# Chunk steps of an RWKV-and-experts kernel cut at another place: the shared down projection, ranks and scatter of a chunk finished in the step after

## The reference, cut to what matters

```python
def wkv(w, u, k, v):                      # a scan over time, per channel
    def step(carry, kv_t):
        aa, bb, pp = carry
        ...
        y = (e1 * aa + e2 * vt) / (e1 * bb + e2)
        ...
xk = xn * att_mix_k + xx * (1.0 - att_mix_k)          # xx: xn one token earlier; xv, xr alike
k, v = xk @ Wk.T, xv @ Wv.T
rwkv = sigmoid(xr @ Wr.T) * wkv(time_decay, time_first, k, v)
x = x + rwkv @ Wo.T
kf = square(relu(xk2 @ Wk_ffn.T))                     # channel mix, 256 -> 1024
x = x + sigmoid(xr2 @ Wr_ffn.T) * (kf @ Wv_ffn.T)
...
shared = (gelu(xf @ w1s) * (xf @ w2s)) @ w3s          # for all tokens
idx = argmax(xf @ Wg, axis=-1)                        # one of 8 experts for each token
final[t] = (gelu(xf @ W1[idx]) * (xf @ W2[idx])) @ W3[idx]
out = x + layernorm(shared + final)
```

## Time and profile before

| | |
|---|---|
| time, median of 3 runs | 1040.57 us (1040.02 to 1044.66) |
| the profiled execution | 1038.19 us, of it span 1036.5 us |
| PE busy | 934.1 us, 90% of the span |
| DVE busy | 760.0 us, 73% |
| ACT busy | 589.9 us, 57% |
| POOL busy | 591.9 us, 57% |
| start of step 3, 15, 16, of the first slot's matmuls | 124.41, 594.93, 633.73, 700.89 us |

### The profile page before, as it was taken

One profiled execution on the slowest core, in us unless ns is written; L12 is line 12 of the kernel. 1 busy time (PEld: TensorE's weight loads), 2 busy tenths in 40 slices (PEclk: granted clock), 3 DMA queues, 4 the chain that ended last, 5 costly groups with the idle time before them and its releaser, 6 DMA issues.

```text
span 1036.5 us, 28181 instructions
## 1 busy us (share of the span) xinstructions
PE 934.1 (90%) x9734; PEld 834.5 (81%) x9734; DVE 760.0 (73%) x1665; ACT 589.9 (57%) x1014; POOL 591.9 (57%) x802
## 2 busy tenths in 40 slices
PE   2388899999999999999999998879999999999994
PEld 1266788788788788888888887758999999999994
DVE  6989999999999999999999986433444444444442
ACT  5477678678678687687687675423333333333331
POOL 6346577577577577577587543234454554555553
PEclk9698999999999999999999999999999999999998
DMA  6113241341341441441443134766877788485510
GB/s 233 61 52 96 111 151 58 137 155 53 129 162 47 136 162 41 142 162 41 142 162 123 56 150 161 249 231 216 266 228 241 249 269 267 146 290 184 193 55 22
DMA packets 87330, 156.26 MB, mean 151 GB/s; under 512 B 5549, under 2 KB 68142, under 8 KB 82160
## 3 DMA queue, kind: packets, MB, share of 16 engines
q1 hardware_dynamic: 35760, 72.74, 20.5%
q10 hardware_dynamic: 46960, 65.89, 19.6%
q0 software_dynamic: 4560, 16.98, 4.3%
HBM read 178.35 MB, written 50.51 MB: 221 GB/s over the span
## 4 chain that ended last, share of the span: by engine, by line
PE 46%; DVE 18%; issue 10%; POOL 9%; ACT 7%; DMA 1%; ACTq 1%; DVEq 0%; POOLq 0%
PE up L334 9%; PE up L335 9%; PE up L336 9%; PE yp L334 4%; PE yp L335 4%; PE yp L336 4%; PE yp L538 2%; PE yp L541 2%; DVE mixed L988 2%; ACT ex L699 2%; POOL inv L1448 2%; DVE gu L1181 2%; DVE er L1058 1%; DVE arena L963 1%; POOL sh_s L1529 1%
## 5 line engine op out<-in xcount | busy, mean ns | idle before, releaser
L334 PE MATMUL up<-mix_s,arena 128*128 128x128 f16 x1248 | 211.1, 219 | 1.5 <-DMA arena<-w_split 1.5
L335 PE MATMUL up<-mix_s,arena 128*128 128x128 f16 x1248 | 211.1, 219 | 0.0
L336 PE MATMUL up<-mix_s,arena 128*128 128x128 f16 x1248 | 211.1, 219 | 0.0
L1529 POOL TENSOR_TENSOR sh_s<-gu,sh_s 128x512 f16<-128x512 f32 x64 | 84.1, 1316 | 141.5 <-ACT sh_s L762 141.5
L334 PE MATMUL up<-xf_s,arena 128*128 128x256 f16 x512 | 139.5, 272 | 1.1 <-DVE gu L1181 1.1
L336 PE MATMUL up<-xf_s,arena 128*128 128x256 f16 x512 | 139.5, 273 | 0.0
L335 PE MATMUL up<-xf_s,arena 128*128 128x256 f16 x512 | 139.5, 272 | 0.0
L1634 POOL TENSOR_TENSOR kf_s<-ex,kf_s 128x512 f16<-128x512 f32 x78 | 90.2, 1157 | 85.4 <-ACT kf_s L922 85.3
L1401 DVE SCALAR_TENSOR_TENSOR ex<-up,ex 128x512 f32<-128x512 f32 x78 | 54.0, 692 | 101.6 <-ACT ex L916 101.2
L334 PEld LDWEIGHTS up<-mix_s,arena 128*128 128x128 f16 x1248 | 122.1, 98 | 2.0 <-DMA arena<-w_split 1.7
L335 PEld LDWEIGHTS up<-mix_s,arena 128*128 128x128 f16 x1248 | 122.1, 98 | 0.4
(11 more groups left out here) (228 smaller groups left out, 2932.1 us busy)
## 6 DMA issues: line engine op xcount, KB each, us to landing
arena<-w_split ACTq DMA_DIRECT2D x117, 1024.0 KB
arena<-in_W SPq DMA_DIRECT2D x24, 1024.0 KB, 7.4
w_split<-arena SPq DMA_DIRECT2D x24, 1024.0 KB, 9.0
rows<-routed_rows ACTq DMA_DIRECT2D x39, 261.0 KB, 2.9
routed_rows<-x_in SPq DMA_DIRECT2D x8, 650.0 KB, 8.3
normed<-routed_rows ACTq DMA_DIRECT2D x39, 128.0 KB, 2.5
x_in<-in_x SPq DMA_DIRECT2D x16, 256.0 KB, 2.8
x_res<-in_x SPq DMA_DIRECT2D x16, 256.0 KB, 2.7
```

What stands on the lines that cost most here:

```text
L334: pe.matmul(out, stat(0), mov(0), start=first, stop=False)
L335: pe.matmul(out, stat(0), mov(1), start=False, stop=False)
L336: return pe.matmul(out, stat(1), mov(0), start=False, stop=last)
L1529: pool.tensor_tensor(sh_s[:, 1, 2 * g:2 * g + 2, :], gu[g % GUS][:], sh_s[:, 0, 2 * g:2 * g + 2, :], ALU.subtract).then_inc(S("sh_lo"), 1)
```

## The change

The step begins at another place. What a step did last for chunk c2, most of `shared_down`, `ranks`, `placing` and `scatter`, is now done early in the next step, as c3 = i - 3; only in the last two steps is it still done at once. `shared_down` is cut into five parts q: part 0 stays in the old step, ahead of `shared_up(3)`; parts 1 to 3 (6 matmuls each) and part 4 (24) stand between the projections and the transposes of the next. `carry` is parted from `tops` and done a step ahead. A late piece's low part and store move one step on. And on every engine the calls within a step are put in another order. The arithmetic is the same.

```diff
@@ sync
-                for e, m in early_piece(i, p, h) + late_piece(i, p, h):
+                for e, m in early_piece(i, p, h) + last_late(i, p, h) + late_now(i, p, h):
                     store_expert(e, m)
@@ tensor
+                before = c3 if not at_step(i, NC + 1) else -1
                 projection(0)
+                projection(1)
                 transpose_normed2()
+                ranks(before)
+                shared_down(before, 1)
+                projection(2)
+                shared_down(before, 2)
+                shared_down(before, 3)
                 transpose_xf()
-                projection(1)
-                projection(2)
-                gate()
-                shared_gate(0)
+                shared_down(before, 4)
                 if at_step(i, NC + 1):
...
+                else:
+                    shared_gate(0)
+                    gate()
+                shared_up(0)
                 shared_gate(1)
-                shared_up(0)
+                receptance()
                 shared_up(1)
-                receptance()
-                channel_mix_up(0)
-                channel_mix_up(1)
                 transpose_next()
...
+                for q in range(4):
+                    channel_mix_up(q)
                 if at_step(i, NC):
...
+                    ranks(c2)
+                for q in range(4):
+                    channel_mix_down(q)
+                output()
+                shared_gate(2)
+                shared_up(2)
+                shared_gate(3)
+                if not at_step(i, NC) and not at_step(i, NC + 1):
+                    shared_down(c2, 0)
+                shared_up(3)
...
+                if at_step(i, NC) or at_step(i, NC + 1):
+                    for q in range(PAIRS + 1):
+                        shared_down(c2, q)
@@ scalar
                 own(0)
                 xn2T_norm()
+                value()
+                if not at_step(i, NC + 1):
+                    xf(c2, p)
+                above(0)
                 xf_hi()
-                above(0)
-                value()
-                exps(0)
-                receptance()
                 above(1)
                 mix2_hi(1)
                 mix2_hi(0)
+                exps(0)
+                receptance()
+                if not at_step(i, -1):
+                    ln0(i + 1, 1 - p)
                 exps(1)
                 own(1)
                 gelu(0)
                 gelu(1)
-                if not at_step(i, -1):
-                    ln0(i + 1, 1 - p)
+                xnT_norm()
                 relu_up(0)
+                if not at_step(i, NC + 1):
+                    y_shared(c3, 1 - p, h + p - 2)
...
                 if at_step(i, NC):
+                    xf(c1, 1 - p)
@@ vector
                 if on(c0):
-                    carry_and_top(c0)
+                    tops(c0)
+                if on(c3) and not at_step(i, NC + 1):
+                    placing(c3, 1 - p, h + p - 2)
...
+                if on(c1):
+                    halo(xn2T, c1, 1 - p, "halo2", "xn2T")
+                if on(c0):
                     distances(c0)
                 own(3)
-                if on(c1):
-                    halo(xn2T, c1, 1 - p, "halo2", "xn2T")
                 if on(i + 1) and not at_step(i, -1):
                     ln0_moments(i + 1)
-                xf_lo()
                 if on(c1):
                     mix2(c1, 1 - p)
+                xf_lo()
...
-                if on(c0):
-                    scan_b(c0)
-                if not at_step(i, NC + 1):
                     early_lo(i, p, h)
                 if on(c1):
                     mix2_lo(c1, 1)
                     mix2_lo(c1, 0)
+                late_lo(last_late(i, p, h))
                 if on(c0):
                     kept(c0)
+                    scan_b(c0)
+                    scan_a(c0)
                 shared(0)
                 shared(1)
...
@@ gpsimd
                 delta2_of()
                 inverse0()
                 now_of()
+                delta_of()
+                scatter(c3, 1 - p)
                 scatter_expert_input()
                 sh_lo(0)
...
                 mix_lo(0)
                 mix_lo(1)
+                sh_lo(1)
+                inverse2()
+                offset2()
                 inverse1()
                 mix_lo(2)
+                sh_lo(2)
+                inverse3()
+                sh_lo(3)
```

More of the change, by code:

```diff
@@ L556, in output, with shared_down @@
                     m.then_inc(S("wo_mm"), 1)
-                def shared_down():
-                    if not on(c2):
+                def shared_down(c, q):
+                    if not on(c):
                         return
-                    if at_step(i, 2):
+                    if at_step(c, 0) and q == 0:
                         pe.wait_ge(S("piece_lo"), N_OWN)
-                    wait(pe, S("x3a"), c1 + 1 if on(c1) else NC)
-                    token_major(yp[1], sh_s, lambda s, k: shared_w[:, 2, s, k * C:(k + 1) * C], FT, "sh_dn_mm",
-                                lambda g: wait(pe, S("sh_lo"), PAIRS * c2 + g + 1))
+                    if q == 0:
+                        wait(pe, S("x3a"), c + 2 if not at_step(c, NC - 1) else NC)
+                    if q < PAIRS:
+                        wait(pe, S("sh_lo"), PAIRS * c + q + 1)
+                    for f in (2 * q, 2 * q + 1) if q < PAIRS else range(FT):
+                        t = q // PAIRS
+                        m = three(pe, yp[1][:, t, :], lambda s: sh_s[:, s, f, t * P:(t + 1) * P],
+                                  lambda s: shared_w[:, 2, s, f * C:(f + 1) * C], f == 0, f == FT - 1)
+                    if q == PAIRS:
+                        m.then_inc(S("sh_dn_mm"), 1)
@@ L1266, in step @@
                     mix0(i + 1, 1 - p, 1)
-                if on(c2) and not at_step(i, NC) and not at_step(i, NC + 1):
-                    gate(c2)
-                if not at_step(i, NC):
-                    late_lo()
+                if on(c1):
+                    x3_gate(c1)
+                if on(i + 1):
+                    carry(i + 1)
+                if on(c1):
+                    x3_sum(c1)
                 if on(i + 1):
@@ L1286, in step @@
                     x2_moments(c0)
+                shared(2)
+                if on(c1):
+                    x1_sum(c1, 1 - p, h + p - 1)
+                    if at_step(i, NC):
+                        x1_moments(c1, 1 - p)
+                shared(3)
                 if on(c1) and not at_step(i, NC):
-                    x1_sum(c1, 1 - p, h + p - 1)
                     x1_moments(c1, 1 - p)
-                if on(c2) and not at_step(i, NC + 1):
+                if at_step(i, NC):
                     placing(c2, p, h - 1)
-                if at_step(i, NC - 1):
-                    zeros_after()
                 if on(c1):
```

192 lines of the change are left out of this document (76 added, 116 removed).

## The result

The changed kernel takes 1076.3 us (median of four runs, 1065.6 to 1082.1), the kernel before, run beside it, 1040.5 (1040.0 to 1044.7). The ratio is 1.026 (95% interval 1.023 to 1.029), without the two of the four runs (1082.0 and 1082.1) that lie over 1.5% above the fastest. The change makes the kernel slower, and by more than twice what was forecast. The profiled execution took 1065.56 us, its span is 1063.8; against the 1038.19 of before that is +27.4, where +10.3 was forecast. What makes up the rest of the +35.8 between the medians stays open; the mean granted clock over the span is lower in the other three, 0.946 to 0.951 against 0.955.

A forecast was written before the change was run, and what follows sets the result against it. TensorE and VectorE, nearly full at 37.3 and 37.4 us per inner step, bound the kernel. 1038.2 + 9.8 - 1.5 + 2 + 0 = 1048.5, 2.4 more for the median: 1051; range 1027 to 1064.

The forecast's parts named there:

- The waits of the earlier trace: TensorE's waits for the transposes of `rows` and for `sh_s`, 1.8 us per inner step, would go.
- TensorE's first idle: Sign: in an inner step it lies ahead of `up<-mix_s,w_fk`, put down to ACT's `gu`.
- the chain behind it: GpSimd's held `inverse0` delays ACT's `ln0`, `exps(1)`, table and Gelu; 4.3 us from inverse to Gelu; steps alternate.
- The work behind `channel_mix_up(0)`: TensorE's work in an inner step once it is ready for that call: 19.8 us.
- The hole: TensorE stands ahead of `channel_mix_up(0)`, 2.1 us, odd steps 4.3; net +0.8 per step, +9.8 in twelve.
- the place of the inverse when the split begins: GpSimd's second power was taken to meet VectorE's split every time; `inverse0` done 2.15 us after the row ends.
- rival (b): GpSimd's second power slips in ahead of the split, two products left: mean step 38.5, time 1033; chance 0.20.
- Rival (c): TensorE's clock falls behind odd-step holes if Gelu comes over 4 us late in one piece: +10, 1061; chance 0.13.
- VectorE's work: VectorE's busy time in the twelve inner steps, 449.30 us, taken as work that bounds a step near 37.4.
- The lock: A row of VectorE instructions with both inputs in SBUF holds a small GpSimd operation throughout: 4.0 us in the row.
- Rival (a): Each VectorE instruction's end in the row lets one GpSimd operation in: -18, time 1023; chance 0.12.
- The edges: Step 1's halo wait +2, step 2 0, step 16 gain -1.6 against deferred matmuls 0 to +4.6; together 0 beyond step 1.

The follow-up runs named there:

- e1: The changed kernel with ACT's `ln0` back behind both `gelu` and TensorE's transposes of `normed` behind `channel_mix_up(1)`: 1029.5 us, ratio 0.988.
- e2: The changed kernel with both expert splits moved out of VectorE's row, the early one behind the four scans, the late one behind `den_now`: 1037.1 us, ratio 0.996.
- e9: The changed kernel with 24 repeated `receptance` matmuls laid around the transposes of `normed` in odd steps only: 1048.7 us, ratio 1.010.
- e5: The changed kernel with the late piece's split moved out of VectorE's row to behind `den_now`: 1042.4 us, ratio 1.001.
- e7: The kernel of e1 with step 1's halo of `xn2T` put back behind `distances` and the own split: 1027.1 us, ratio 0.986.
- e10: The kernel of e1 with 24 repeated `receptance` matmuls in each step that has the channel mix: 1064.5 us, ratio 1.023.

## Why the prediction was wrong, point by point

**Right.** The change is slower, as the forecast had it. The waits of the earlier trace rows went. TensorE's first idle moved ahead of `up<-mix_s,w_fk`, put down to ACT's `gu`, with a smaller one just ahead of it, at the transposes of `normed`; the chain behind it (held operation, `ln0`, `exps(1)`, table, Gelu) and its alternation of even and odd steps are those forecast, and e1 and e2 each take the hole away by cutting one link of it. The work behind `channel_mix_up(0)`, 19.8 us, is exact: 225.33 to 245.10 in step 5, 185.51 to 205.31 in step 4.

**The hole, over-priced.** The forecast was 19.1 and 21.3 us from the step's start to `channel_mix_up(0)`, steps of 38.9 and 41.1. At clock 1.00 it is 18.2 and 20.0, and steps of 37.9 and 39.8, mean 38.8. The term that was mis-sized is the place of the inverse when the split begins: I chose to have the power left behind the row, and in steps 3 to 7 it had slipped in ahead of it, as rival (b) had it (38.5). By that alone the change gains 12 x 0.4 = 4.6 us where the sum has a loss of 9.8 (by its own steps, 40.0 against 39.21, it is 9.5).

**The clock, left out of the sum: this is the step that failed.** The sum prices all twelve inner steps at full clock, +9.8; they cost +19.7 (490.2 against 470.5), at a mean clock of 0.94 from step 7 to 13. Rival (c) named the mechanism, but gave it 0.13 and +10 us. It let the fall wait for more than 4 us of Gelu's lateness in one piece, and argued that the transposes of `normed` split the hole. The trace shows that splitting did not help: the second piece is 2.29 in step 5 and in step 7, only the first differs (0.50 and 0.75), and that decided; 0.86 and 2.20 were enough in step 8. A fall was priced at 1.65 us, from a stretch of 3.3 us in the ramp. Here matmuls ran at half speed for 29.9 us in seven steps, the even ones included, which cost half of that, 15.

And the rival stopped there: it did not ask what the slower TensorE moves. The engines' order in time shifts, more of `inverse0` meets the row, and the next hole is longer: 3.05 us in the even steps 8, 10 and 12, where steps 4 and 6 have 0.92, and 4.26 in step 9. That is what lets the clock fall in the even steps, as e9 shows. The odd steps don't need it: in step 7 the clock fell with no fall ahead of it, and steps 11 and 13 have a hole like its own (3.03, 3.04 in step 7). The holes of steps 7 to 13 come to 22.6 us, where at the lengths of steps 3 to 6 they would be 13.9. Against seven steps at 38.8 the seven cost 25.8: an estimate from these rows has about 15 of them for the clock, 9 for the longer holes, the rest open. With all twelve steps at 38.8 the changed kernel would be at 1065.6 - 490.2 + 466.0, some 1041, no change; e5, which comes nearest to that, is at 1042.4. The forecast had the sign by luck: its reason, the hole at full clock, would by itself have been worth nothing.

**VectorE's work, over-counted.** The prediction took VectorE's busy time, 449.30, for work that bounds a step at 37.4. In e1 the same work, less twelve instructions of 0.06 us, is 421.42, 35.1 per step: `val<-val,er` (128x512), for one, takes 0.68 us there and 1.48 in the kernel before. So part of that busy time was no work of VectorE's own; what lengthened it no run tests.

**The lock.** Rival (a), that each end of a VectorE instruction lets one operation in, is out: the power of 6.68 us passed four such ends. The Trainium skill ("SBUF — State Buffer", "Who interferes with whom") has the loser wait for the whole instruction of the other; the trace shows a wait for the whole row, and the measurement decides. The row ended at the scans; these read SBUF as well (`state<-ex,state`), and why they let GpSimd in stays open.

**The edges, under-priced.** Steps 0 to 2 cost 3.1 (forecast 2). The wait of 3.0 us that was named is there, but by e1 and e7 putting the halo back returns 0.9 of step 1's 3.6; `ln0`'s old place returns 2.9 of them. This number came near for a reason that is mostly another. From step 15 to the slots the change costs 4.9, where the forecast had -1.5 and 0: the deferred matmuls arrive in step 16, as bounded (0 to +4.6), and there a low part meets a split, which the forecast did not look for: it lasts 2.1 us longer, and TensorE waits 3.7 for it.

The range, 1027 to 1064, missed both the median and the profiled execution. It took rival (c) as +10 on the forecast, and had no case in which falls lengthen the holes behind them.

## What to carry to other kernels

Ask of every hole that a reorder makes in TensorE not only how long it is but whether the granted clock holds behind it, and don't count on a few short matmuls to split it: here two idle pieces with four transposes between them let the clock fall. If it may fall, give that a price in the sum, and follow what the shift does to the next step. Here a chain of tiny GpSimd instructions beside a row of VectorE instructions with both inputs in SBUF could end only behind the row. On the engine that waits for the chain's result, put urgent work ahead of that wait (e1), or shorten the row (e2, e5). To test whether the clock is the cost, put useless matmuls into the hole: a kernel that gets faster by more work speaks for the clock, above all if the same matmuls cost time where there is no hole (e10).

## What the runs showed of the hardware that was not expected

- The clock's fall lay between holes that differ by 0.25 us: 0.50 and 2.29 us of idle with 0.66 of transposes between kept 1.00 (step 5), 0.75 and 2.29 gave 0.51 in the 6 us behind it (step 7).
- A GpSimd operation that alone takes 0.7 us lasted 6.68 beside five VectorE instructions in a row with both inputs in SBUF (step 9), and one of 1.16 us lasted 3.25 beside a single split of 2.28.
- 144 more matmuls (15.7 us of TensorE's time) made the twelve inner steps 21 us shorter (469.2 against 490.2), laid into the holes of the six odd steps, behind four of which (7, 9, 11 and 13) the clock had fallen.
